# Moving the last group's projection work, and the first loads of the next phase, into the state stage of a one-core language-model tower

## What is computed

```python
h = embed(x) * 16                                  # [32, 128, 256]
n = layernorm(h)
x1 = n @ w1.T + b;  x_conv = silu(depthwise_conv(x1))      # 3 taps along the sequence
x_ssm = ssm(x_conv, A, B, C, D)                    # h = h*sigmoid(A) + x*B;  y = sum(h*C) + D*x
v = silu(n @ v1.T + b)
h = h + (x_ssm * v) @ w2.T + b2
m = layernorm(h)
shared = (silu(m @ sw1 + sb1) * (m @ sw3 + sb3)) @ sw2 + sb2
routed: two experts a token, chosen by (11*token + 7919*k) % 8;  gelu(m @ w1[e] + b1) @ w2[e] + b2
h = h + (shared + routed/2) / 2
```

## Time and profile before

| | us |
|---|---|
| median of 3 runs (lowest, highest) | 440.6 (439.9, 441.26) |
| the profiled execution | 440.82 |
| its span, first to last instruction | 439.0 |
| busy in the span: PE, DVE, ACT, POOL | 400.8, 275.9, 243.4, 212.7 |
| mean granted TensorE clock (of 1) | 0.984 |

### The profile page before, as it was taken

One profiled execution on the slowest core, in us unless ns is written; L12 is line 12 of the kernel. 1 busy time (PEld: TensorE's weight loads), 2 busy tenths in 40 slices (PEclk: granted clock), 3 DMA queues, 4 the chain that ended last, 5 costly groups with the idle time before them and its releaser, 6 DMA issues.

```text
span 439.0 us, 8388 instructions
## 1 busy us (share of the span) xinstructions
PE 400.8 (91%) x2880; PEld 351.4 (80%) x2880; DVE 275.9 (63%) x607; ACT 243.4 (55%) x438; POOL 212.7 (48%) x237
## 2 busy tenths in 40 slices
PE   3879899899998883999999999999999999998996
PEld 2767788788678871788898988988988988887885
DVE  6667998889757689474565565565554654655333
ACT  4567878778876363635535635635635536535442
POOL 7678988831009166558337247247247336433000
PEclk9999999999999897799999999999999999999999
DMA  2533111299959962101111211201301301100101
GB/s 63 156 95 135 49 61 57 70 288 308 299 160 245 255 235 96 50 0 43 52 52 48 55 43 49 73 22 48 95 0 49 96 0 48 48 0 0 49 0 48
DMA packets 32779, 38.86 MB, mean 89 GB/s; under 512 B 3461, under 2 KB 29027, under 8 KB 32624
## 3 DMA queue, kind: packets, MB, share of 16 engines
q1 hardware_dynamic: 29616, 32.99, 24.1%
q0 software_dynamic: 3136, 5.52, 4.4%
HBM read 34.56 MB, written 8.65 MB: 98 GB/s over the span
## 4 chain that ended last, share of the span: by engine, by line
PE 69%; DVE 16%; ACT 6%; issue 5%; POOL 2%; DMA 1%; DVEq 0%; ACTq 0%; POOLq 0%
PE ps L1174 20%; PE ps L1175 20%; PE ps L1176 20%; DVE hid_lo L1107 3%; PE ps L1257 3%; DVE stat L985 2%; PE ps L1293 1%; DVE h2n L998 1%; PE ps L1212 1%; DVE v_sb L1061 1%; PE ps L1259 1%; PE ps L1182 1%; DVE catT_lo L978 1%; DVE act_out L1101 1%; DVE x_mid L1038 1%
## 5 line engine op out<-in xcount | busy, mean ns | idle before, releaser
L1107 DVE SCALAR_TENSOR_TENSOR hid_lo<-act_out,hid_hi 128x512 fp32r<-128x512 f32 x64 | 54.9, 859 | 58.9 <-ACT hid_hi L891 58.9
L878 ACT ACTIVATE act_out<-ps,vec 128x512 f32<-128x512 f32 x32 | 22.1, 689 | 89.7 <-PE ps L1176 89.7
L1101 DVE SCALAR_TENSOR_TENSOR act_out<-ps,vec,act_out 128x512 f32<-128x512 f32 x32 | 24.0, 751 | 53.7 <-ACT act_out L878 53.7
L701 POOL TENSOR_TENSOR h_sb<-h_sb,bias_e 128x256 f32<-128x256 f32 x32 | 24.3, 764 | 53.6 <-DVE h2n L998 53.6
L1176 PE MATMUL ps<-h2nT_hi,sw_lo 128*128 128x512 f32 x128 | 50.0, 391 | 0.0
L1175 PE MATMUL ps<-h2nT_lo,sw_hi 128*128 128x512 f32 x128 | 50.0, 391 | 0.0
L1174 PE MATMUL ps<-h2nT_hi,sw_hi 128*128 128x512 f32 x128 | 49.9, 390 | 0.0
L694 POOL TENSOR_TENSOR zc_lo<-v_sb,zc_hi 128x256 fp32r<-128x256 f32 x32 | 29.2, 912 | 36.5 <-ACT zc_hi L868 36.5
L882 ACT ACTIVATE act_out<-ps,vec 128x512 f32<-128x512 f32 x32 | 22.0, 689 | 41.2 <-PE ps L1176 41.0
L550 POOL DMA_INDIRECT cat<-table_dram,x_ids x32 | 36.6, 1144 | 8.4 <-issue 6.0
L891 ACT ACTIVATE hid_hi<-act_out 128x512 fp32r<-128x512 f32 x64 | 39.7, 622 | 0.0
(11 more groups left out here) (134 smaller groups left out, 1258.5 us busy)
## 6 DMA issues: line engine op xcount, KB each, us to landing
toep_l<-kernel_rows_dram SPq DMA_DIRECT2D x14, 512.0 KB, 7.3
toep_r<-kernel_rows_dram SPq DMA_DIRECT2D x12, 512.0 KB, 7.6
h_rows_dram<-h_ring SPq DMA_DIRECT2D x32, 128.0 KB, 2.2
h_in<-h_rows_dram SPq DMA_DIRECT2D x8, 512.0 KB, 4.4
stage<-w_e_dram POOLq DMA_DIRECT2D x7, 512.0 KB, 3.6
out_dram<-o_sb SPq DMA_DIRECT2D x7, 512.0 KB, 3.2
bias_e<-rows_dram SPq DMA_DIRECT2D x1, 1024.0 KB, 6.8
toep_r<-kernel_rows_dram SPq DMA_DIRECT2D x4, 256.0 KB, 6.0
```

The costliest lines, as they stand in the source:

```text
L701: nc.gpsimd.tensor_tensor(at, at, bias_e[:, bass.ds(e, 1), :].rearrange("p o c -> p (o c)"), ALU.add).then_inc(h2_biased, 1)
L878: nc.scalar.activation(act_out[:, n % 4, :], ps[bank][:, :], ACT.Silu, bias=vec[:, C_SB1 + j:C_SB1 + j + 1]).then_inc(act_done, 1)
L1101: nc.vector.scalar_tensor_tensor(act_out[:, n % 4, :], ps[bank + 1][:, :], vec[:, C_SB3 + j:C_SB3 + j + 1], act_out[:, n % 4, :], ALU.add, ...
L1107: nc.vector.scalar_tensor_tensor(hid_lo[:, n % 4, :], act_out[:, n % 4, :], 0.5 if kind == SHARED else 0.25, f32(hid_hi[:, n % 4, :]), ALU ...
```

## The change

The last group (and it alone) projects its four x units first, half 0 of D ahead of half 1, then v. Two of its v units, of half 1, leave phase A: TensorE computes them behind steps 3 and 7 of the state stage (`LATE_V`). The turns of the last two x units, and their casts, stand inside the state stage too; one of them uses the bank of `HNP`. `y_sb` is laid out half by half, since hnT and the projection weights are still in use when it is written first. SyncE loads the b2 row (into `first_row`, a part of `stage`), h_in(0) and pieces 1 and 2 behind a wait for all projections, ahead of the loads for steps 14 and 15, and h_in(1), piece 3 and, after both h_in are biased, piece 4 behind them. The first expert is two pieces, so there are ten. ScalarE casts pieces 1 to 4 behind the copies of steps 8 to 11; GpSimd subtracts pieces 1 to 4 and biases both h_in before the first mixer. The fourth mixer group of the first slot gets a bank of its own.

```diff
+LAST_PROJ = [(X1, 0), (X1, 2), (X1, 1), (X1, 3), (V, 0), (V, 2), (V, 1), (V, 3)]
+LATE_V = {3: 6, 7: 7}
@@ SBUF
-    h_in = sb(ctx, "h_in", [P, 2, GROUPS, D], F32, L)
+    h_in (moved behind sw_lo);  wv_hi, wv_lo (moved behind hnT)
+    first_row = stage[:, 1:2, 0:D]
-    y_sb = sb(mem_y, "y_sb", [P, BATCH, D], F32, L)
+    y_sb = sb(mem_y, "y_sb", [P, HALVES, BATCH, P], F32, L)
@@ w2_bank
-        return ps[(4, 5, 6, 4)[g] if isinstance(e, int) and e == 0 else 6]
+        return ps[(4, 5, 6, 3)[g] if isinstance(e, int) and e == 0 else 6]
@@ pieces
-    LO_BY = (1, 1, 0, 0, 0, 0, 0, 0, 1)
+    LO_BY = (1, 1, 1, 1, 1, 0, 0, 0, 0, 1)
@@ SyncE
         for q in range(TRING, NQ):
+            if q == TRING + 4:
+                sp.wait_ge(mm_done, 8 * GROUPS)
+                w2_row_in(first_row)
+                h_load(0, 0)
+                piece_in(1)
+                piece_in(2)
             sp.wait_ge(ssm_done, 2 * (q - TRING + 1))
             toep_load(q)
+        h_load(1, 1)
+        piece_in(3)
+        sp.wait_ge(h_biased, 2)
+        piece_in(4)
...
         sp.wait_ge(bias_step, BIAS_STEPS)
+        w2_row_in(w2_bias)
+        sp.wait_ge(ssm_done, 2 * (NQ - 2))
+        for n in range(5, 9):
             piece_in(n)
         sp.wait_ge(w_lo_done[1], 3)
-        piece_in(8)
+        piece_in(9)
@@ GpSimd
+        pool.wait_ge(ssm_done, 1)
+        bias_steps()
         pool.wait_ge(rows_in, 48)
-        add_w2_bias(0, 1)
-        first_expert_lo(0)
+        add_w2_bias(0, 1, first_row)
+        add_w2_bias(1, 1, first_row)
+        for n in range(1, 5):
+            piece_lo(n)
         for g in range(GROUPS):
             mixer_lo(0, g)
-        first_expert_lo(1)
         for g in range(GROUPS):
             power_step(g, g, eps2_done, rstd2_done)
-        add_w2_bias(1, 1)
@@ ScalarE
         for q in range(NQ):
+            if q == 0:
+                act.wait_ge(x_turned, 4 * GROUPS)
             for bank in range(2):
                 act.wait_ge(ssm_done, 2 * q + bank + 1)
                 nc.scalar.copy(y_at(q, bank), y_part(q, bank, 1)).then_inc(y_low, 1)
+            if q in (0, 2):
+                x_hi_part(GROUPS - 1, 2 + q // 2, last_one=True)
+            if q in LATE_V:
+                out_(GROUPS - 1, LATE_V[q], late=True)
+            if q in (8, 9, 10, 11):
+                piece_hi(q - 7)
@@ VectorE
+            if q in (0, 2):
+                x_lo_part(GROUPS - 1, 2 + q // 2, last_one=True)
...
         for u in range(8, 16):
             z_part(u)
-        piece_lo(2)
-        piece_lo(3)
...
-        piece_lo(4)
         turn2_lo(0, 0, 3)
-        piece_lo(5)
-        piece_lo(6)
-        piece_lo(7)
+        for n in range(5, 9):
+            piece_lo(n)
@@ TensorE
-        pe.wait_ge(x_lo_done, 15)
+        pe.wait_ge(x_lo_done, 14)
...
             if q == 0:
+                x_turn(GROUPS - 1, 2, last_one=True)
                 x_turn(GROUPS - 1, 3, last_one=True)
+            if q in LATE_V:
+                project(GROUPS - 1, LATE_V[q], late=True)
```

More of the change, by code:

```diff
@@ L63, with is_last, projection, x1_at @@
 X1_AT = [PROJ.index((X1, g)) for g in range(4)]
+LAST_PROJ = [(X1, 0), (X1, 2), (X1, 1), (X1, 3), (V, 0), (V, 2), (V, 1), (V, 3)]
+LATE_V = {3: 6, 7: 7}
+def is_last(i):
+    return isinstance(i, int) and i == GROUPS - 1
+def projection(i, at):
+    return (LAST_PROJ if is_last(i) else PROJ)[at]
+def x1_at(i, n):
+    return n if is_last(i) else X1_AT[n]
+def x1_part(i, n):
+    g = projection(i, x1_at(i, n))[1]
+    return g // 2, g % 2
 def slot_of(r):
@@ L224, in _tower @@
     z_done = sem("z_done")
-    piece_sem = [sem(f"piece_in{n}") for n in range(9)]
+    piece_sem = [sem(f"piece_in{n}") for n in range(10)]
     w_hi_done = sem("w_hi_done")
@@ L282, in add, with behind @@
                 out_.append((name, i - back if back else i, index))
-        def behind(name, r, lag, positions=range(RES)):
-            at = (r - 3 - lag) % RES
+        def behind(name, r, lag, x1=False):
+            at, back = (r - 3 - lag) % RES, 1 if r >= 3 + lag else 2
+            group = i - back if isinstance(i, int) else None
+            positions = [x1_at(group, n) for n in range(4)] if x1 else range(RES)
             if at in positions:
-                add(name, 1 if r >= 3 + lag else 2, positions.index(at))
+                add(name, back, positions.index(at))
         for r in range(RES):
@@ L315, in phase_a @@
                 add("hn", 0, (r - 4) // 2)
-            behind("x", r, 3, X1_AT)
-            behind("silu", r, 2, X1_AT)
+            x_behind = isinstance(i, int) and i == GROUPS and r >= 6
+            if not x_behind:
+                behind("x", r, 3, True)
+            behind("silu", r, 2, True)
             add("mm", 2, 5 + r) if r < 3 else add("mm", 1, r - 3)
+            if x_behind:
+                behind("x", r, 3, True)
         return out_
@@ L373, in y_at @@
     def y_at(q, bank):
-        first = q * CH + bank * CH // 2
-        return y_sb[:, :, first:first + CH // 2]
+        first = q % (NQ // 2) * CH + bank * CH // 2
+        return y_sb[:, 1 - q // (NQ // 2), :, first:first + CH // 2]
     def yt_bank(u):
@@ L664, in link, with bias_steps @@
             pool.wait_ge(bias_step, steps)
[L666 to L673, removed]
+        def bias_steps():
+            pool.wait_ge(bias_scaled, 5)
+            link(nc.gpsimd.tensor_copy(bias_row[:, 1, :], bias_e[:, RES - 1, :]))
+            for e in range(RES - 1, -1, -1):
+                before = bias_e[:, e - 1, :] if e else bias_row[:, 1, :]
+                link(nc.gpsimd.tensor_tensor(bias_e[:, e, :], bias_e[:, e, :], before, ALU.add))
+                link(nc.gpsimd.tensor_tensor(bias_e[:, e, :], bias_e[:, e, :], bias_row[:, 0, :], ALU.add))
+            assert steps == BIAS_STEPS
         def expert_in(n, par):
@@ L826, in hn_hi, with x_hi_part, out_ @@
             nc.scalar.copy(hnT_at(hnT_hi, i, pair), hn_bank()).then_inc(hnT_hi_done, 1)
-        def x_hi_part(i, u):
+        def x_hi_part(i, u, last_one=False):
+            if is_last(i) and u >= 2 and not last_one:
+                return
             need(act, x_turned, 4 * i + u + 1)
-            nc.scalar.copy(x_at(x_hi, i, u), x_bank()).then_inc(x_hi_done, 1)
-        def out_(i, at):
-            kind, g = PROJ[at]
+            nc.scalar.copy(x_at(x_hi, i, u), x_bank(i, u)).then_inc(x_hi_done, 1)
+        def out_(i, at, late=False):
+            kind, g = projection(i, at)
+            if is_last(i) and at in LATE_V.values() and not late:
+                return
             need(act, mm_done, 8 * i + at + 1)
@@ L904, in slot @@
                     turn2_hi(e + 1, 1 - par, n - 3)
-        piece_hi(1)
+        piece_hi(5)
+        piece_hi(6)
         for g in range(GROUPS):
@@ L1058, in z_part @@
             half, k = u // 8, u % 8
+            if k == 6 and half == 0:
+                dve.wait_ge(mm_evac, 8 * GROUPS)
             dve.wait_ge(yt_filled, u + 1)
@@ L1206, in x_turn, with project @@
         def x_turn(i, u, last_one=False):
-            if isinstance(i, int) and i == GROUPS - 1 and u == 3 and not last_one:
+            if is_last(i) and u >= 2 and not last_one:
                 return
             need(pe, sil_done, 4 * i + u + 1)
-            need(pe, x_lo_done, 4 * i + u)
+            if is_last(i) and u == 3:
+                need(pe, hnT_lo_done, 4 * GROUPS)
+            else:
+                need(pe, x_lo_done, 4 * i + u)
             for b in range(4):
-                last = nc.tensor.transpose(XP[:, b * P:(b + 1) * P], x_sil[:, u, b, :], ident[:, :])
+                last = nc.tensor.transpose(turn_bank(i, u)[:, b * P:(b + 1) * P], x_sil[:, u, b, :], ident[:, :])
             last.then_inc(x_turned, 1)
-        def project(i, at):
-            which, g = PROJ[at]
+        def project(i, at, late=False):
+            which, g = projection(i, at)
+            if is_last(i) and at in LATE_V.values() and not late:
+                return
             k, half = g // 2, g % 2
@@ L1274, in mixer_mm @@
             need(pe, zc_lo_done, n + 1)
-            if isinstance(e, int) and e == 0:
-                need(pe, h2_done, g - 2)
-            else:
+            if not isinstance(e, int) or e:
                 need(pe, h2_done, n)
```

97 lines of the change are left out of this document (47 added, 50 removed).

## The result

| | before | after |
|---|---|---|
| median of the runs, us (lowest, highest) | 440.6 (439.9, 441.31) | 444.93 (444.1, 446.06) |
| ratio, 95% interval | | 1.0096 [1.0084, 1.0108] |
| the profiled execution's span, us | 439.0 | 443.3 |
| mean granted clock | 0.984 | 0.973 |

The kernel is 4.3 us slower; 444.2 was forecast. The change does what it says: the state stage starts 3.1 us earlier, and the transition is 3.8 us shorter. Both are more than spent inside the state stage.

What follows compares the result with a forecast made beforehand. TensorE was taken as busy nearly throughout, with VectorE's chain the bound from 157.4 to 176.2 us. State stage +7.2, slow turns +0.3 and transition -3.9 gave +3.6 on 440.6: 444.2 us, range 437.5 to 448.5.

Steps and rivals of the forecast that it cites:

- one sign of being right: State stage: TensorE idle before steps 13 and 14 by about 10 us in all.
- Start of the stage: State stage: with x first and two v units moved, it starts at 126.65 instead of 130.02, 3.4 us earlier.
- Steps 0 to 7 with the late v: State stage: eight steps, two x turns and two v units end at about 139.4, when SyncE's wait ends.
- The loads: DMA queue behind SyncE's wait: h_in(1) lands at 153.0, with 266 GB/s taken from the trace.
- its own case of a full backlog: DMA queue: with the full backlog of earlier loads, h_in(1) lands at 154.0.
- The casts: State stage, ScalarE: casts waiting for pieces hold the y copies; z run 7.0 to 7.4 us later, 7.2 taken.
- the right branch: End of state stage: step 14 through the last add takes 4.3 us at the lower clock, 3.4 at full clock.
- The transition: z run to first expert: splits moved gain 1.8 us, second h_in add moved 2.0; -3.9 with the transpose.
- The sum: Whole kernel: +7.2, +0.3 and -3.9 give +3.6 us, 444.2 us.
- the quick queue: Rival, DMA queue: h_in(1) lands before break-even at 149.4, at 148.4 for 348 GB/s; 437.6 to 439.6 us; chance 0.22.
- that rival: Transition: the clock stays up, with the queue as forecast, 2.0 us less, 442.2 us; chance 0.12.
- the late start: Rival, state stage: ScalarE's four x parts run late, start stays at 130, +3.4, 447.6 us; chance 0.11.

Runs made afterwards that it cites:

- r5: r4 with GpSimd's second h_in add ahead of its splits of pieces 3 and 4, without the wait for the last h2n: 437.63 us, ratio 0.9918 to before.
- r4: The kernel after with no cast in the state stage, SyncE's loads reordered (ring loads first) and GpSimd's second h_in add behind the last h2n: 435.24 us, ratio 0.9874.
- r1: The kernel after with ScalarE's casts of pieces 1 to 4 moved behind the state stage, SyncE's order untouched: 440.91 us, ratio 0.9997 to before.
- r3: The kernel after with the b2 row loaded once into its final place, so piece 4 doesn't wait for the h_in adds: 442.53 us, ratio 1.0039.
- r6: r4 with all four v units of the last group computed ahead of the state stage: 438.33 us, ratio 0.994 to before.
- r7: r4 with the casts of pieces 1 and 2 put back into the state stage, behind the copies of steps 12 and 13: 438.91 us, ratio 0.9949.
- r2: The kernel after with the loads of steps 14 and 15 issued ahead of the wait for the projections, casts still inside the stage: 445.02 us, ratio 1.0092.

## Why the prediction was right, step by step

The prediction was right in its mechanism, the casts that wait inside the stage, and in its sum. The date of h_in(1) came out well by luck (point 3), and one sign of being right failed (point 4).

1. *Start of the stage.* Walked to 126.65, measured 126.90 (before 130.02). ScalarE's order and VectorE's last x_lo decide it, as put.
2. *Steps 0 to 7 with the late v.* 139.4 forecast for the release of SyncE; its first issue behind the wait is at 139.91, 0.5 late, half of it from the start.
3. *The loads.* h_in(1) landed at 153.8 (145.62 and 8.17), 153.0 forecast. From 139.9 to 153.9 the queue moved 296 GB/s, not 266: the rate was taken low. Against that the queue was freed late. The last load for steps 10 to 13 was issued at 134.57 and took 8.7 us, so it landed at 143.3 and not at 142.2, and the forecast had also gone 1.0 us below its own case of a full backlog (154.0). Behind it the queue moved 314 GB/s until 153.8. The errors nearly cancel, and that is luck. By the 341 GB/s of the Trainium skill ("DMA: Bandwidth & Descriptors", section on measured bandwidth) the estimate was near 148.6; the trace doesn't agree, by 5.2 us. The page measured loads issued from GpSimd; these are issued by SyncE, behind others.
4. *The casts.* Right in mechanism and place. The end of the chain was put at 164.3 to 164.5 and measured 165.06. The distribution was off: stalls of 2.5, 7 and 3 us forecast for TensorE, 3.75, 3.11 and 2.37 measured, before steps 11, 13 and 14. One of the signs of being right therefore failed: before steps 13 and 14 TensorE was idle for 5.5 us, not for about 10. The steps between ran at half the clock, so that they filled what had been put down as idle. From 146 us to 152 the clock is near 0.5 and again from 156 to 166 (0.61 in its first two microseconds). So 4.3 us, at the lower level, was the right branch: step 14 to the z run took 4.4 us. The end was right because one chain sets it, whatever happens between.
5. *The transition.* 3.9 us less was forecast, 18.88 - 15.03 = 3.85 was measured. r5 shows the 2.0 of the collision; the other 1.8 was not tried alone, but the first h2n comes at 173.54, 8.5 us behind the z run's start instead of 10.3.
6. *The sum.* +3.6 forecast, +4.3 measured in span and medians; +3.9 of it stands at the first expert's first matmul. The term that was too small is step 4's, by 0.6 us (7.2 forecast, 165.06 - 157.28 = 7.8 measured). Where the last 0.4 behind 180 us went is not settled: it is no more than the medians can tell.

The rivals: the quick queue would have needed h_in(1) by 149.4. The clock fell in the transition too (0.50 from 178 to 182 us in after), so that rival fell; so did the late start, by the 126.90. What the prediction didn't see is how much the rest of the change can give: r4 gains 5.6 us on before, with x first, the late v and y by halves untouched. It takes more than removing the casts, which alone (r1) only brings back the time of before; the loads, the other casts and GpSimd's work had to be put in order too.

## What to carry to other kernels

Before a step that waits for a load is put into an engine's queue in the middle of a tight stage, ask what stands behind it in that queue and who waits for that: here four casts of 0.62 us each cost 4.4 us of the kernel (r1). Taking them out is half of the cure. If what they wait for still comes late, the wait moves into the next stage; with the loads and their users put in order as well, the change gains 5.6 us on before (r4). A load that is issued only after another engine's use of its place makes a serial chain (landing, addition, issue, landing, cast), and one such chain in front of the stage's own work sets the end; r3 cut one link out of it and gained 2.5 us. Date the pieces by bytes queued ahead of them at the rate the trace shows for that mixture, and place their use behind that date.

## What the runs showed of the hardware

TensorE stalls in the middle of a step, with no releaser in the profile, in most kernels whose stage isn't held otherwise: 1.87 us in before, 0.93 in r4, 1.74 in r5, 2.15 in r6, 1.14 in r7, none in r1. The stages of r4 and r5 have the same program, so the length of the stall differs between executions (or chips) of one and the same stage. In all five an instruction packet of about 0.02 MB stands in the DMA record within four microseconds ahead of it, among data loads at a share near 1.0. That suggests instructions fetched behind queued data, but r1 has such a packet at 146 to 148 too and no stall, and no run separates it. What can be said is its price: after the stalls of 1.87, 1.74 and 2.15 us the granted clock fell to 0.50 for about 3 us, after those of 0.93 and 1.14 it did not.

```profile
144.00:146.00 2.00, 1.63 (x39) 1.55 (x37) 1.87 (x5) 0.75 (x2) 0.00 (x0) 1.00 0.95 188
146.00:148.00 2.00, 1.44 (x34) 1.44 (x34) 0.83 (x2) 0.60 (x2) 0.00 (x0) 1.00 0.96 213
148.00:150.00 2.00, 2.00 (x47) 2.00 (x45) 1.90 (x5) 1.05 (x4) 0.00 (x0) 1.00 1.06 352
```

These three stretches are r4's; r6's stand above. When VectorE and GpSimd collide, it is mostly VectorE that pays here. A normalization of 256 columns takes 0.41 us alone and 2.42 beside GpSimd's addition, which takes its 2.34 either way (2.35 in after, alone). Four splits take 2.49 alone (after) and 6.26 beside GpSimd's work in r4, where the addition grows only to 2.83. But z, whose first operand lies in PSUM, keeps its 0.6 us each beside GpSimd: 6.06 for ten in r4, with GpSimd's add and splits at 153.30 to 158.1, and 6.06 in r2, where GpSimd is idle until the first zc_lo at 168.15.
